# Three tiles to a signal in the one-hot segment sum: PE, VectorE and the gathers of a graph kernel

## What is computed

```python
x = _layernorm(x + _L0_gnn_ref(x, edge_index, conv_w, conv_b, lin_w, lin_b))
...
W = jnp.einsum('rb,bio->rio', w_comp, bases)          # 8 relations from 4 bases
msg = x[edge_src] * edge_norm[:, None]
seg = edge_type * N + edge_dst
agg = jax.ops.segment_sum(msg, seg, num_segments=R * N).reshape(R, N, -1)
out = jnp.einsum('rni,rio->no', agg, W)
x = _layernorm(x + out)
```

## Time and profile before

| | us |
|---|---|
| median of 3 runs (1859.42 to 1873.81) | 1865.01 |
| the profiled execution | 1863.87 |
| its span, first to last instruction | 1862.1 |
| PE matmuls busy in the span | 1147.9 (62%) |
| GpSimd busy in the span | 820.8 (44%) |
| VectorE busy in the span | 792.9 (43%) |

### The profile page before, as it was taken

One profiled execution on the slowest core, in us unless ns is written; L12 is line 12 of the kernel. 1 busy time (PEld: TensorE's weight loads), 2 busy tenths in 40 slices (PEclk: granted clock), 3 DMA queues, 4 the chain that ended last, 5 costly groups with the idle time before them and its releaser, 6 DMA issues.

```text
span 1862.1 us, 18954 instructions
## 1 busy us (share of the span) xinstructions
PE 1147.9 (62%) x6042; PEld 841.1 (45%) x6042; DVE 792.9 (43%) x1636; ACT 257.6 (14%) x630; POOL 820.8 (44%) x931
## 2 busy tenths in 40 slices
PE   2478999999982455555554555565545455555446
PEld 2455666455471344344443434444434333444445
DVE  3798996455661333233332232333323323333324
ACT  3498894002030000000000000000000000000000
POOL 4220000000006666665555656655556556556562
PEclk8679999999995656556655655656565656656666
DMA  4500001001112111111111111111111111111110
GB/s 126 178 15 2 1 1 35 1 1 35 35 27 88 43 45 42 47 45 41 41 39 41 42 41 45 48 39 41 38 41 45 39 44 47 41 41 44 39 44 24
DMA packets 51315, 77.86 MB, mean 42 GB/s; under 512 B 18282, under 2 KB 35159, under 8 KB 50628
## 3 DMA queue, kind: packets, MB, share of 16 engines
q0 software_dynamic: 26512, 54.60, 10.6%
q1 hardware_dynamic: 24756, 22.61, 4.1%
HBM read 65.48 MB, written 6.88 MB: 39 GB/s over the span
## 4 chain that ended last, share of the span: by engine, by line
PE 43%; another core or an unknown queue 19%; DVE 16%; issue 14%; DVEq 3%; DMA 2%; POOL 1%; ACT 1%; SPq 0%; ACTq 0%; POOLq 0%
PE ps L1252 24%; PE ps L1145 13%; DVE arena L1012 6%; DVE arena L865 4%; DVEq L1012 2%; PE ps L1265 2%; PE ps L1258 2%; PE ps L1134 1%; PE ps L1232 1%; DVE arena L1021 1%; DVE arena L1020 1%; PE ps L1161 1%; DVE arena L847 1%; POOL arena L627 1%
## 5 line engine op out<-in xcount | busy, mean ns | idle before, releaser
L1252 PE MATMUL ps<-arena 128*128 128x192 f32 (+9 forms) x2200 | 616.9, 440 | 562.2 <-DVE arena L1012 413.0
L661 POOL DMA_INDIRECT arena<-x_scratch,arena x806 | 761.6, 945 | 241.0 <-issue 233.7
L1252 PEld LDWEIGHTS ps<-arena 128*128 128x128 f32 x2200 | 489.3, 291 | 694.2 <-DVE arena L1012 500.2
L1012 DVE SCALAR_TENSOR_TENSOR arena<-ps,arena 128x192 f32<-128x192 f32 x806 | 323.6, 416 | 877.4 <-remote 389.2
L1145 PE MATMUL ps<-arena,u 125*128 125x480 fp8e5 (+1 forms) x1575 | 359.7, 353 | 0.5 <-ACT arena L721 0.5
L1145 PEld LDWEIGHTS ps<-arena,u 125*128 125x128 bf16 x1575 | 151.0, 97 | 103.8 <-ACT arena L721 1.0
L865 DVE TENSOR_TENSOR arena<-arena 128x2048 bf16<-128x2048 bf16 (+2 forms) x158 | 188.7, 1254 | 11.0 <-PE ps L1134 7.2
L778 ACT ACTIVATE arena<-arena,epst 128x1 f32<-128x1 f32 x25 | 7.4, 294 | 1293.4 <-issue 891.9
L642 POOL IOTA arena<- 128x48 f32 x1 | 0.2, 176 | 396.0 <-PE ps L1145 396.0
L1134 PE MATMUL ps<-arena 128*128 128x125 bf16 x1256 | 149.0, 233 | 33.8 <-DVE arena L865 31.8
L1134 PEld LDWEIGHTS ps<-arena 128*128 128x128 bf16 x1256 | 107.0, 104 | 85.4 <-DVE arena L865 49.6
(11 more groups left out here) (124 smaller groups left out, 507.2 us busy)
## 6 DMA issues: line engine op xcount, KB each, us to landing
arena<-x_scratch,arena POOLq DMA_INDIRECT x806
arena<-hT SPq DMA_DIRECT2D x3, 1562.5 KB, 7.1
arena<-in_x_dram SPq DMA_DIRECT2D x2, 1562.5 KB
edge_scratch<-arena SPq DMA_DIRECT2D x5, 403.0 KB, 6.1
arena<-edge_scratch SPq DMA_DIRECT2D x4, 403.0 KB, 15.2
dinv_all<-dinv_scratch SPq DMA_DIRECT2D x1, 1562.5 KB, 13.8
h_scratch<-hT SPq DMA_DIRECT2D x1, 1562.5 KB, 11.0
out_dram<-arena SPq DMA_DIRECT2D x24, 64.0 KB
```

The lines of the kernel that those rows point to most:

```text
L661: nc.gpsimd.indirect_dma_start(out=gat[:, j, :], out_offset=None, in_=x1_d, in_offset=bass.IndirectOffsetOnAxis(ap=idxg[:, j:j + 1], axis= ...
L1012: V.scalar_tensor_tensor(mov[:, j % MS, :, :], ps[:, 4:5, 0:WN].broadcast_to([P, NB, WN]), dl[:, ds(c * TPB + j, 1)], coef[:, ds(c * TPB + ...
L1252: last = T.matmul(o, gat[:, j, :], mov[:, j % MS, :, a - LO[j]:b - LO[j]], start=False, stop=False, skip_group_check=True)
```

## The change

The sum is the same, tile for tile. Three tiles now form a batch (`BT = 3`, 11 batches to a chunk, `TB`). PE signals once behind a batch, VectorE once behind the three one-hots of a batch, and each batch of gathers has its own semaphore, for which PE waits at the batch's first tile. VectorE has room for four batches, twelve one-hots (`MS = 4`), in place of three one-hots. The gathers are issued in groups of 12, 12 and 9 (`GB`), and GpSimd no longer waits for PE: it waits for the indices alone, and VectorE copies these at points where it has itself seen that PE is done with the places: group 0 of the next chunk after the one-hots of batch 7, group 1 after the first batch of the new chunk, group 2 behind `fold`. The row of 48 places is read from PSUM bank 4 as before. `finish` moves from tile 12 to tile 14, `stats` and `norm` to batches 6 and 7.

```diff
-                    for g in range(-(-count // GG)):
+                    for g in range(sum(1 for a in GB if a < count)):
                         pool.wait_ge(s_idx, 3 * c + g + 1)
-                        if not first:
-                            pool.wait_ge(s_mu, TPB * c - TPB + GG * (g + 1))
                         pool.wait_ge(s_x1d, 16 * NUB)
...
-                        for j in range(GG * g, min(count, GG * (g + 1))):
+                        for j in range(GB[g], min(count, GB[g + 1])):
                             nc.gpsimd.indirect_dma_start(out=gat[:, j, :], out_offset=None, in_=x1_d,
-                                                         in_offset=bass.IndirectOffsetOnAxis(ap=idxg[:, j:j + 1], axis=0)).then_inc(s_g[g], 16)
+                                                         in_offset=bass.IndirectOffsetOnAxis(ap=idxg[:, j:j + 1], axis=0)).then_inc(s_g[j // BT], 16)
...
-                def moving(c, j, first):
-
-                    if not first:
-                        dve.wait_ge(s_mu, c * TPB + (j - MS + 1))
-                    V.scalar_tensor_tensor(mov[:, j % MS, :, :], ps[:, 4:5, 0:WN].broadcast_to([P, NB, WN]),
...
+                def moving(c, q, head, n=BT):
+
+                    if q >= MS:
+                        dve.wait_ge(s_mu, c * TB + (q - MS + 1))
+                    elif not head and q < TB % MS:
+                        dve.wait_ge(s_mu, c * TB - (TB % MS - 1 - q))
+                    for i in range(n):
+                        ins = V.scalar_tensor_tensor(mov[:, q % MS, i, :, :], ps[:, 4:5, 0:WN].broadcast_to([P, NB, WN]),
...
+                        if i == n - 1:
+                            ins.then_inc(s_m, 1)
...
+                    at_stats, at_norm = (6, 7) if count == TPB else (4, 4)
+                    for q in range(-(-count // BT)):
+                        moving(c, q, head, min(BT, count - BT * q))
+                        if q == 1 and not head:
                             fold(c - 1)
+                            indices(c, 2, count)
+                        if q == 0 and not head:
+                            indices(c, 1, count)
...
+                        if q == 7:
+                            indices(c + 1, 0, following)
...
-                    if j % GG == 0:
-                        pe.wait_ge(s_g[j // GG], c * (16 * GG) + 16 * min(GG, count - j))
-                    pe.wait_ge(s_m, c * TPB + (j + 1))
+                    q = j // BT
+                    if j % BT == 0:
+                        pe.wait_ge(s_g[q], c * (16 * BT) + 16 * min(BT, count - j))
+                        pe.wait_ge(s_m, c * TB + (q + 1))
...
-                    last.then_inc(s_mu, 1)
+                    if j % BT == BT - 1 or j == count - 1:
+                        last.then_inc(s_mu, 1)
```

53 lines of the change are left out of this document (24 added, 29 removed).

## The result

The changed kernel takes 1925.3 us (median of four runs, 1923.6 to 1925.8) against 1865.8 us (four runs, 1859.4 to 1873.8): the ratio is 1.0315, with a 95% interval of 1.0274 to 1.0356. I had forecast 1704 us. Later runs showed that this result holds where PE's signals come late, as they did in the run whose rows I had read. On other chips they come promptly; there the kernel before takes 1596 us and the changed one 0.2% less.

The account below looks back on a forecast made before the run. It took delayed PE signals, a toll on each while gathers are in flight, as the bound: first fold 615, 23 chunks of 46.2 us (1063), 24 for the last, 1.8 around it, 1704 us; range 1588 to 1790.

Parts of the forecast that it names:

- The toll per signal: PE's signals to VectorE: each pays a delay, in order, while gathers are in flight, some 4.2 to 4.9 us.
- the 46.2 us: Forecast chunk length: 7 us of prompt signals, nine signals at 4.2 us (37.8), and 1.4 at the chunk border.
- The 14% between tiles of two and four MATMULs: Signal intervals on PE, 4.90 against 5.60 us: read as hardly different, so against a price per matmul.
- nothing is gained but chunk 0: Rival: price lies on matmuls or tiles, chunk stays 52.15 us, 1838 us, or 1864 with chunk 0 unchanged; chance 0.10.
- Lateness alone is covered: VectorE's twelve one-hots on hand equal 15 us of gathers, so a signal 12.5 us late costs nothing; only signal rate counts.
- GpSimd's slack of 20 to 26 us: Index copies releasing GpSimd: their conditions are met 20 to 26 us early, enough for up to five delayed signals.
- the moved `stats` and `norm`: VectorE's statistics and normalisation at later batches: worth nothing, since they lie under the gathers.
- Chunk 0: First chunk of the second sum: it ends with its gathers, first fold at 615 us instead of 640.72, 25 us off.
- The rival on the slower side: Gathers without GpSimd's pauses drive signal intervals to 5.6 us: chunk 57.1 us, 1954 us in all; chance 0.07.
- The mark that I had named for "wrong": Sign of failure: a batch's first one-hots over 5 us apart throughout, and GpSimd pausing over 10 us per chunk.
- The rule on the end of a matmul: TensorE's traced ends are estimates and signals follow PSUM's acknowledgement, so the 12.5 us could be matmuls really ending late.
- The tolls vanish: Rival: signal delay falls with the number of signals, gathers set the pace at 41.5 us per chunk, 1594 us; chance 0.32.

Follow-up runs that it names:

- sig_tile: Changed kernel with PE's signal behind every tile again, 33 to a chunk, batches and gathers as they are: 1926.7 us.
- half_cols: Changed kernel with each matmul of a tile over two of the four bases, 96 columns and not 192, same number of MATMULs and signals: 1913.7 us.
- border: Changed kernel with a PSUM bank centred on the chunk border, 66 MATMULs a chunk instead of 90, and row numbers copied before `stats` and `norm`: 1846.8 us, 0.984 of before.
- a_bf16: Changed kernel with tile products from the operands' upper two bytes, one MATMUL and one LDWEIGHTS instead of two each: 1799.6 us, 0.959 of the kernel before.
- idx_early: Changed kernel with VectorE's copy of the next chunk's first twelve row numbers moved ahead of `stats` and `norm`: 1831.0 us, 0.976 of before; repeated 1832.8 us, 0.9795.
- set 3: Group of follow-up runs, edits of the changed kernel, on one chip with prompt signals; the kernel before took 1595.8 us beside them.
- set 6: Group of follow-up runs, edits of the changed kernel, on one chip with late signals; the kernel before took 1866.3 us beside them.
- after_again: The changed kernel itself, unaltered, run once more on a chip with prompt signals: 1593.1 us, 0.9980 of the kernel before.
- pool_plain: Changed kernel with each indirect gather replaced by a plain DMA of 128 rows from the same GpSimd queue: 1021.3 us.
- pace1_2: Changed kernel with a small GpSimd addition ahead of every gather in place of each group's marker, late signals: 1924.8 us, 1.031 of the kernel before.

## Why the prediction was wrong

*The toll per signal* is the step that failed. "PE gives 11 tile signals per chunk and not 33", nine of them at 4.2 us, made the 46.2 us. sig_tile (33 signals, 1926.7 us) shows that signals have no price. In the earlier trace rows a signal, a tile and two to four MATMULs were the same thing, and I chose the signal. The 14% between tiles of two and four MATMULs, which I took as evidence against a price of matmuls, says little: half_cols shows that the delay doesn't follow columns, and border and a_bf16 that it follows instructions weakly, if at all. What the changed kernel shows in its place is a batch signal every 11 to 16 us during the gathers of chunk 0, three times the 4.2 to 4.9 of a tile, and in a steady chunk none for 33 us, until the gathers pause. Calculated with three times the toll, the "rivals" case "nothing is gained but chunk 0" was the right price, and I gave it 0.10.

*"Lateness alone is covered"* by twelve one-hots held only while signals are at most 15 us late. The join waits 30.5 us: with unbroken gathers the signal came after their end, so the lateness grew with the burst. And the one-hots on hand don't cover the join, which needs batch 1 and stands ahead of all further one-hots in VectorE's queue.

*GpSimd's slack of 20 to 26 us* was counted in tolls of 4 to 5 us; at 11 to 16 us it holds one or two, and with a signal that waits for the pause none. And I had not seen that what stands ahead of the copy on VectorE adds to GpSimd's pause: the text names the condition that "the index copies carry" but not the twelve one-hots, `stats` and `norm` between join and copy, 8.7 us per chunk. idx_early brought these down to 4.5 us and turned the loss of 3.2% into a gain of 2.0%. I had put the moved `stats` and `norm` at nothing; they stand ahead of the copy, and that decides the sign.

*Chunk 0* was to end at 615 us and ended at 634.1, with batch signals 11 to 16 us apart in place of one toll of 4.9. On a chip with prompt signals it ended at 609.2.

*The rival on the slower side* ("by gathers without a pause", 0.07) has the mechanism that took place: no wait on PE in GpSimd's queue, long runs of gathers, signals that come some 4 us after the last one. It gave 57.1 us per chunk and 1954 us; measured were 54.9 and 1925. Its "interval" per signal was wrong too, and its 57.1, of a drain, four batches and a fold, came close by luck: the steady chunk is 41.5 of gathers, 5.5 to drain and 8.7 of VectorE's queue, 55.7; the average is less because chunk 1 and the last ones are shorter. The mark that I had named for "wrong", GpSimd pausing over 10 us per chunk, is met, 14.4 us; but it was a weak mark, since the 11.8 us before the change pass it too.

*The rule on the end of a matmul.* I set the Trainium skill (Perfetto Trace Analysis, on the per-engine timelines) aside because PE's starts went on in order. That argument was too quick: half_cols shows the starts themselves held up, 2.1 to 2.8 us apart, after some 33 MATMULs. A start in the rows says nothing of when those ahead are done, so the rows never excluded that the matmuls complete late. Whether the completion or only its signal is late, no run here tells.

*"The tolls vanish"* at 1594 us (0.32) is the time on a chip with prompt signals, 1593.1 us, within a microsecond. That is luck and not the mechanism: no toll vanished by the change, since there the kernel before has this time too.

**What stays open.** Why one kind of chip delays TensorE's signals beside indirect gathers and another doesn't. The number of the chip in the records doesn't settle it: set 3 (prompt) and set 6 (late) carry the same number, so it may be a condition of the chip or its machine and not the chip. Also open is which part of the indirect form does it, and the exact law of the delay: not per signal, not per column, and not in proportion to the instructions. One more difference stands in the traces: of the 12896 landings that the gathers' semaphores count, the trace of the changed kernel records 2119 where signals are late, and all but three where they are prompt (after_again); for pool_plain, in a set with late signals, it has them all. So the delay may be bound up with how signals, or the records of them, are delivered. Every execution on record has a profiled span and clock, so no run tells whether the delay is there without the profiler.

## What to carry to other kernels

Where an engine's signal comes late and the releaser has no name, don't count what it signals before an experiment has told signal, instruction and neighbour apart: the three are one and the same in a kernel that signals once per tile. Taking away a wait that makes an engine pause can lengthen the delay which the pause was flushing; and when the wait is handed to another engine's queue, everything ahead of the release in that queue is added to it, so the releasing copy belongs first. idx_early is the version to keep: 0.98 of the kernel before where signals are late, and by its structure no different from the changed kernel where they are prompt (it wasn't run there).

## What the runs showed of the hardware

- While GpSimd issues indirect gathers of 128 rows back to back (1.25 us apart), the join waits up to 34.3 us for TensorE's signal on some chips; on others, with the same code, 5.0 us at most. The kernel before takes 1866 us on the former and 1596 us on the latter.
- In steady chunks the join's delayed signal arrives a fixed time after the last gather: 5.3 to 5.5 us in the changed kernel, 3.1 to 3.4 in pace1_2, 5.5 to 5.7 in half_cols. With fewer instructions (a_bf16) it arrives while gathers run.
- Plain DMAs of the same size and number, from SyncE's queue (128 GB/s) or from GpSimd's (0.53 us each), delay nothing, in the sets in which the gathers do. The Trainium skill (SBUF — State Buffer, Who interferes with whom) says that a DMA never contends with a compute engine and that PE and ACT never wait on anyone. The plain DMAs here agree; beside the indirect ones PE's starts and signals are held up (single MATMULs 2.1 to 2.8 us apart in half_cols), for a reason that the runs don't show, while VectorE's one-hots take 0.409 us each where signals are late and where they are prompt.
